# End of a mixed attention and expert kernel rearranged: stores ahead of the last heads, last sums inverted turned, last projection in parts, 71 expert tiles

## What is computed

```python
xn = layernorm(x)
# attention: 16 heads of 8 channels, rotary positions, causal
q, k, v = xn @ Wq.T, xn @ Wk.T, xn @ Wv.T
scores = q @ k.T / sqrt(8)                 # per head, upper triangle masked
att = softmax(scores) @ v
out_a = att @ Wo.T
# experts: 8, each row goes to its best two
probs = softmax(xn @ router_w.T);  top_w, top_idx = top_k(probs, 2)
top_w = top_w / (sum(top_w) + 1e-9)
h = relu(xn @ w1[e].T + b1[e]);  y = h @ w2[e].T + b2[e]
out_f = sum over the two of y * top_w
result = x + out_a + out_f
```

## Time and profile before

| | |
|---|---|
| median of 3 runs | 703.01 us (701.86 to 705.95) |
| the profiled execution | 699.11 us |
| its span, first to last instruction | 697.3 us |
| mean granted TensorE clock in it | 0.988 |
| busy: PE, PE weight loads, DVE, ACT, POOL | 93%, 54%, 80%, 66%, 37% |
| DMA | 69.34 MB, 99 GB/s over the span |

### The profile page before, as it was taken

The page is one execution under the profiler, slowest core; times in us unless marked ns, Lnnn a source line. Parts: engine busy times, 40 slices in busy tenths (PEclk is TensorE's granted clock), DMA queues, the critical chain, the costliest instruction groups (busy, mean ns, idle before and its releaser), DMA issues.

```text
span 697.3 us, 18181 instructions
## 1 busy us (share of the span) xinstructions
PE 651.8 (93%) x5925; PEld 376.8 (54%) x5925; DVE 554.9 (80%) x1306; ACT 463.3 (66%) x994; POOL 257.3 (37%) x308
## 2 busy tenths in 40 slices
PE   8699979999999999999999999999999998998995
PEld 3455534443443443447999999964344344343543
DVE  6956789999999798796666666679989988999424
ACT  3364207777778778777666666657777776777571
POOL 2556502217556556541000000024544544545350
PEclk9979999999999999999999999999999999999999
DMA  9499973146476355142322222271633626136034
GB/s 243 122 214 218 218 202 46 34 73 121 105 132 123 80 118 97 49 92 71 94 69 68 68 68 70 68 145 38 94 57 57 90 45 80 28 86 162 18 93 120
DMA packets 63660, 69.34 MB, mean 99 GB/s; under 512 B 8974, under 2 KB 51470, under 8 KB 63530
## 3 DMA queue, kind: packets, MB, share of 16 engines
q1 hardware_dynamic: 59464, 60.06, 39.5%
q0 software_dynamic: 4096, 8.40, 5.0%
q10 hardware_dynamic: 34, 0.02, 0.0%
HBM read 41.11 MB, written 26.67 MB: 97 GB/s over the span
## 4 chain that ended last, share of the span: by engine, by line
PE 34%; DVE 14%; issue 3%; DMA 3%; SPq 1%; ACT 0%; POOL 0%; DVEq 0%; POOLq 0%; ACTq 0%
PE bank L1441 9%; PE bank L1459 9%; DVE mx L922 9%; PE bank L1390 5%; PE bank L1355 4%; DVE q_high L914 3%; PE bank L1317 2%; DMA k_high<-slots_out_d,slot 1%; PE bank L1450 1%; PE bank L1485 1%; PE bank L1500 1%; DVE xn_all L1049 1%; DMA early<-heads_d 1%; DMA tiles_s<-heads_d 1%; PE bank L1325 1%
## 5 line engine op out<-in xcount | busy, mean ns | idle before, releaser
L794 ACT ACTIVATE probs<-bank 128x512 f32<-128x512 f32 (+2 forms) x640 | 319.3, 554 | 128.2 <-PE bank L1355 120.5
L922 DVE TENSOR_REDUCE mx<-bank 128x2 f32<-128x1024 f32 (+2 forms) x200 | 216.3, 1127 | 20.2 <-PE bank L1325 15.6
L689 POOL TENSOR_SCALAR_AFFINE_SELECT probs<-probs 128x512 f32<-128x512 f32 x128 | 83.6, 654 | 295.9 <-ACT probs L794 294.5
L1390 PE MATMUL bank<-probs,vst 128*32 128x256 f32 (+3 forms) x2432 | 187.0, 380 | 4.0 <-issue 2.9
L1355 PE MATMUL bank<-stack 64*128 64x512 f32 (+3 forms) x768 | 160.4, 417 | 1.3 <-ACT probs L794 0.7
L1317 PE MATMUL bank<-stack 64*128 64x512 f32 (+3 forms) x768 | 140.1, 382 | 16.2 <-DVE mx L922 9.3
L914 DVE CUSTOM_DVE_ANT_0 q_high<-bank,later_s 128x384 bf16<-128x384 f32 (+1 forms) x240 | 136.3, 618 | 17.7 <-PE bank L1317 15.9
L1355 PEld LDWEIGHTS bank<-stack 64*128 64x128 f32 x768 | 74.8, 185 | 110.6 <-ACT probs L794 90.7
L1317 PEld LDWEIGHTS bank<-stack 64*128 64x128 f32 x768 | 71.6, 185 | 59.0 <-DVE mx L922 32.6
L1390 PEld LDWEIGHTS bank<-probs,vst 128*32 128x32 f32 x2432 | 48.5, 108 | 78.0 <-issue 54.6
L672 POOL DMA_INDIRECT k_high<-slots_out_d,slot x64 | 61.3, 958 | 59.4 <-ACT probs L794 54.3
(11 more groups left out here) (138 smaller groups left out, 466.3 us busy)
## 6 DMA issues: line engine op xcount, KB each, us to landing
stack<-parts_d SPq DMA_DIRECT2D x96, 128.0 KB
slots_in_d<-const_s SPq DMA_DIRECT2D x4, 1152.0 KB, 10.6
tiles_s<-slots_in_d SPq DMA_DIRECT2D x72, 64.0 KB, 1.8
slots_out_d<-k_high SPq DMA_DIRECT2D x72, 64.0 KB, 1.6
early<-in_w_experts SPq DMA_DIRECT2D x8, 514.0 KB
stack<-parts_d SPq DMA_DIRECT2D x64, 64.0 KB
parts_d<-probs SPq DMA_DIRECT2D x8, 512.0 KB, 6.2
heads_d<-xnT SPq DMA_DIRECT2D x124, 18.0 KB
```

The source lines that it names most:

```text
L689: pool.affine_select(out=t, in_=t, compare_op=ALU.is_ge, fill=0.0, base=0, pattern=[[0, HG], [1, P]], channel_multiplier=-1).then_inc(s["d ...
L794: nc.scalar.activation(to, src, ACT.Exp, scale=SCALE).then_inc(s["probs_made"], 1)
L922: v.tensor_reduce(to, src.rearrange("p g (a k) -> p g a k", k=w), AX_X, ALU.max, negate=True).then_inc(s["scores_read"], 1)
L1390: last = mm(pv[32 * h:32 * h + 32, begin:end], vst[r % 2][:, kb, h, :], probs[n % 3][:, h, begin:end], start=first_of(n) and begin == 0, s ...
```

## The change

1. `TILES` is 71 instead of 72. With 8192 slots and 8 experts no more than 71 tiles can be in use. The loop over tiles makes 15 rounds of four instead of 16, and seven tiles are written out after it instead of four. The slots that are cleared, the counts that POOL waits for and the two late loads of `acc` (`ACC_AT`) follow.
2. SP issues the stores of sequences 0 and 1 before it stores the first half of unit 15, and it loads the last sequence's heads before it waits for the inverted sums.
3. The last sums are turned first: four matmuls with the 128x128 blocks of `oraw[1]` as weights and four columns give 128x16 in PSUM; DVE inverts 128x16, copies it out to 128x512 in two halves (each value 32 times), PE turns it back with the identity, and DVE multiplies from PSUM in two halves.
4. The last sequence's projection is in three parts of 4, 2 and 2 blocks of rows (`ENDS`), each in a bank of its own, with its own addition and its own store.
5. Their bias rows are issued inside unit 15, behind steps 6, 8 and 9 (`BIASED`), instead of at the end.

```diff
-TILES = SLOTS // P + E
+TILES = SLOTS // P + E - 1
...
-    with eng.Fori(1, TILES // 4 - 1) as i:
+    whole = (TILES - 4) // 4
+    with eng.Fori(1, whole) as i:
         for r in range(4):
             tile(i * 4 + r, r)
-    for r in range(4):
-        tile(TILES - 4 + r, r)
+    for j in range(4 * whole, TILES):
+        tile(j, j % 4)
...
+        ENDS = [(0, CK), (CK, CK + CK // 2), (CK + CK // 2, T)]
+
+        BIASED = {(LAST + 3, 6): 0, (LAST + 3, 8): 1, (LAST + 3, 9): 2}
...
-        ACC_AT = [0, 3, TILES - 4, TILES - 2]
+        ACC_AT = [0, 3, TILES - 3, TILES - 2]
...
+        def last_of_all(i):
+
+            use = place_in_order["project", B - 1, 0]
+            first, end = ENDS[i]
+            col = i % 2 * HALF
+            return ms[(use + i // 2) % 2][:, col:col + (end - first) * C]
...
+                if isinstance(u, int) and u == LAST + 3:
+                    for b in range(B - 2):
+                        store_out(b)
                 store_heads(u, 0)
...
                 if isinstance(u, int) and u == LAST + 3:
-                    for b in range(B - 2):
-                        store_out(b)
                     load_last_sums()
+                    load_last_heads()
                     spread_last()
                     store_out(B - 2)
...
-            dve.wait_ge(s["sums_spread"], 1)
-            v.reciprocal(over_last, st[0]).then_inc(s["over_made"], 1)
+            dve.wait_ge(s["sums_turned"], 1)
+            v.reciprocal(over_turned, st[0][:, 0:CK * HG]).then_inc(s["over_made"], 1)
             dve.wait_ge(s["over_made"], 1)
-            v.tensor_tensor(heads_last, oraw[1], over_last, ALU.mult).then_inc(s["att_ready"], 1)
-            for c in range(2):
-                dve.wait_ge(s["proj_made"], B + c)
+            for i in range(2):
+                some = slice(i * CK * HG // 2, (i + 1) * CK * HG // 2)
+                v.tensor_copy(over_wide[:, i * HALF // 2:(i + 1) * HALF // 2].rearrange("p (a r) -> p a r", r=32),
+                              over_turned[:, some].unsqueeze(2).broadcast_to([P, CK * HG // 2, 32])
+                              ).then_inc(s["turned_made"], 1)
+            for i in range(2):
+                dve.wait_ge(s["sums_spread"], i + 1)
+                cols = slice(i * HALF // 2, (i + 1) * HALF // 2)
+                v.tensor_tensor(heads_last[:, cols], oraw[1][:, cols], st[1 + i][:, 0:HALF // 2], ALU.mult
+                                ).then_inc(s["att_ready"], 1)
+            for i, (first, end) in enumerate(ENDS):
+                dve.wait_ge(s["proj_made"], B + i)
...
+            def bias_last(i):
+
+                use = place_in_order["project", B - 1, 0]
+                first, end = ENDS[i]
+                pe.wait_ge(s["scores_read"], use if i == 2 else use - 1)
+                pe.wait_ge(s["b2_loaded"], 16 * (NT // 2))
+                bt = (B - 1) % 2 * T
+                mm(last_of_all(i), gT[:, (B - 1) // 2, :],
+                   b2_blk[:, bt + first:bt + end, :].rearrange("p t c -> p (t c)"), start=True, stop=False)
...
-            mm(st[0], sum_rows, oraw[1], start=True, stop=True).then_inc(s["sums_spread"], 1)
...
+            pick_sums = sum_rows.rearrange("p (h r) -> p h r", h=HG)[:, :, 0]
+            for t in range(CK):
+                last = mm(st[0][:, t * HG:(t + 1) * HG], oraw[1][:, t * P:(t + 1) * P], pick_sums,
+                          start=True, stop=True)
+            last.then_inc(s["sums_turned"], 1)
+            for t in range(CK):
+                pe.wait_ge(s["turned_made"], 1 + t // 2)
+                last = mm(st[1 + t // 2][:, t % 2 * P:(t % 2 + 1) * P], over_wide[:, t * P:(t + 1) * P], ident,
+                          start=True, stop=True)
+                if t % 2:
+                    last.then_inc(s["sums_spread"], 1)
+            for i, n in ((0, H), (1, H - HG), (2, H - HG)):
+                pe.wait_ge(s["att_ready"], B + min(i, 1))
...
+            for i in (1, 2):
+                pe.wait_ge(s["att_ready"], B + 1 + i)
...
```

More of the change, by code:

```diff
@@ L412, in zero_slots @@
             def zero_slots(i):
-                tiles = slice(i * TILES // 4, (i + 1) * TILES // 4)
+                first, end = i * TILES // 4, (i + 1) * TILES // 4
+                tiles = slice(first, end)
                 sp.dma_start(slots_in_d.rearrange("(j p) c -> p j c", p=P)[:, tiles, :],
-                             zeros.unsqueeze(1).broadcast_to([P, TILES // 4, C])).then_inc(s["slots_zeroed"], 16)
+                             zeros.unsqueeze(1).broadcast_to([P, end - first, C])).then_inc(s["slots_zeroed"], 16)
             def load_stacks(u, r):
@@ L534, in spread_last, with load_last_heads, store_last @@
                         [n, DH, HALF])).then_inc(last_loaded[c], 16)
+            def load_last_heads():
+                for c, u in ((0, UNITS), (1, UNITS - 1)):
+                    n, cols = (u - LAST) * HG, slice(c * HALF, (c + 1) * HALF)
                     sp.dma_start(heads_s[B - 1][0:n * DH, cols], heads_d[LAST:u, :, 0:DH, cols].rearrange(
                         "g h d s -> (g h) d s")).then_inc(last_loaded[c], 16)
-            def store_last(c):
-                sp.wait_ge(s["scores_read"], place_in_order["project", B - 1, 0] + 1 + c)
+            def store_last(i):
+                first, end = ENDS[i]
+                sp.wait_ge(s["scores_read"], place_in_order["project", B - 1, 0] + 1 + i)
                 sp.wait_ge(s["combined"], 2 * NT)
-                t0 = (B - 1) * T + c * CK
-                sp.dma_start(out[t0 * P:(t0 + CK) * P, :].rearrange("(t p) c -> p t c", p=P),
-                             acc[:, t0:t0 + CK, :]).then_inc(s["out_stored"], 16)
+                t0 = (B - 1) * T + first
+                sp.dma_start(out[t0 * P:(t0 + end - first) * P, :].rearrange("(t p) c -> p t c", p=P),
+                             acc[:, t0:t0 + end - first, :]).then_inc(s["out_stored"], 16)
             def store_out(b):
@@ L598, in _ @@
             all_units(sp, unit, experts)
-            for c in range(2):
-                store_last(c)
-            sp.wait_ge(s["out_stored"], 16 * (B + 1))
+            for i in range(len(ENDS)):
+                store_last(i)
+            sp.wait_ge(s["out_stored"], 16 * (B - 1 + len(ENDS)))
         @block.gpsimd
@@ L1423, in unit @@
                         project(PROJECTS[u, j])
+                    if isinstance(u, int) and (u, j) in BIASED:
+                        bias_last(BIASED[u, j])
             LOADS = 2 * 6
@@ L1536, in _ @@
             pe.wait_ge(s["probs_made"], banks_before(UNITS, 0))
-            mm(st[0], sum_rows, oraw[1], start=True, stop=True).then_inc(s["sums_spread"], 1)
-            use = place_in_order["project", B - 1, 0]
-            at = ms[use % 2]
-            pe.wait_ge(s["scores_read"], use - 1)
-            for c, n in ((0, H), (1, H - HG)):
-                pe.wait_ge(s["att_ready"], B + c)
-                ps = at[:, c * HALF:(c + 1) * HALF]
-                bias_rows(ps, B - 1, c)
-                for t in range(CK):
-                    col = (c * CK + t) * P
-                    last = mm(ps[:, t * C:(t + 1) * C], heads_s[B - 1][0:n * DH, col:col + P],
-                              w_proj[0:n * DH, 5, :], start=False, stop=c == 0 and t == CK - 1)
-                if c == 0:
-                    last.then_inc(s["proj_made"], 1)
@@ L1552, in _ @@
-            pe.wait_ge(s["att_ready"], B + 2)
-            for t in range(CK):
-                last = mm(ps[:, t * C:(t + 1) * C], heads_last[:, t * P:(t + 1) * P], w_proj[:, 6, :],
-                          start=False, stop=t == CK - 1)
-            last.then_inc(s["proj_made"], 1)
+            pick_sums = sum_rows.rearrange("p (h r) -> p h r", h=HG)[:, :, 0]
+            for t in range(CK):
+                last = mm(st[0][:, t * HG:(t + 1) * HG], oraw[1][:, t * P:(t + 1) * P], pick_sums,
+                          start=True, stop=True)
@@ new lines, in _ @@
+            last.then_inc(s["sums_turned"], 1)
[7 more added lines that the diff above has]
+                pe.wait_ge(s["att_ready"], B + min(i, 1))
+                first, end = ENDS[i]
+                for t in range(first, end):
+                    to = last_of_all(i)[:, (t - first) * C:(t - first + 1) * C]
+                    last = mm(to, heads_s[B - 1][0:n * DH, t * P:(t + 1) * P], w_proj[0:n * DH, 5, :],
+                              start=False, stop=i == 0 and t == end - 1)
+                if i == 0:
+                    last.then_inc(s["proj_made"], 1)
@@ L1559 @@
+            for i in (1, 2):
+                pe.wait_ge(s["att_ready"], B + 1 + i)
+                first, end = ENDS[i]
+                for t in range(first, end):
+                    to = last_of_all(i)[:, (t - first) * C:(t - first + 1) * C]
+                    last = mm(to, heads_last[:, (t - CK) * P:(t - CK + 1) * P], w_proj[:, 6, :],
+                              start=False, stop=t == end - 1)
+                last.then_inc(s["proj_made"], 1)
```

14 lines of the change are left out of this document (6 added, 8 removed).

## The result

The changed kernel takes 699.21 us in the median of 15 runs (695.29 to 702.32), the kernel before 701.84 us over 15 runs (698.74 to 706.72; the three shown above are among them). The ratio on record, which is not the quotient of these two medians, is 0.9946 with a 95% interval of 0.9921 to 0.9970: 3.8 us faster (2.1 to 5.5), against 4.5 predicted. The medians alone differ by 2.6 us. The profiled execution took 697.34 us.

The account below looks back on a forecast made before the run. PE was taken to bound the expert phase, and a string of small transfers, with attention close beside it, the tail. From the 703.0 us median, −2.0 for the tile and −2.5 at the end gave 698.5 us; range 696.6 to 701.6.

Parts of the forecast that it names:

- the first case: Attention leads the transfers in the tail, as summed: 3.4 to 5.6 us faster, 697.4 to 699.6 us; chance 0.60.
- The tile: Expert phase, bound by PE: one loop round of four tiles becomes three written-out tiles, −2.01 us.
- The moved stores: SP's queue: outputs issued some 10 us earlier, so the sums' load lands in 2.17 instead of 3.67 us, −1.5.
- The other heads ready: Tail's transfer path: with heads loaded early, the other heads' second multiplication ends at 685.3 instead of 688.78 us.
- The bias rows: Unit 15: bias matmuls ahead of scores delay ACT by 1.1 us, bounds 0.3 and 1.7; the third costs nothing.
- The projection row: Profile evidence for the bias price: a projection's two halves take PE 3.5 us, and ACT then idled 4.11 us.
- From the second copy to the end: Last heads copied out at 686.3, then turning, small inversion, products, projection and last store; end at 694.7 or 694.8 us.
- The sum of the tail: Span ends at 694.7 or 694.8 instead of 697.3 us: −2.5 us for all tail edits together.
- The clock rival: PE's clock falls in the tail before the projection: +2.7 us, so −1.8 in all and 701.2 us; chance 0.20.
- Transfers leading: Tail's transfers stay last, other heads ready at about 688.7: −3.2 us in all, 699.8 us; chance 0.10.
- stores not hidden: Moved output stores hold up unit 15's gathers or code loads; ACT loses 3.0 us, 701.5 us; chance 0.06.
- the slower case: PE's clock falls before the last products, doubling the tail's matmuls: +5.9, so +1.4 and 704.4 us; chance 0.04.

Follow-up runs that it names:

- experiment 5: Changed kernel with SP's old order: outputs stored behind the last heads' stores, heads loaded beside the spread sums; 702.84 us in a single run.
- experiment 1: Kernel before with 71 tiles and nothing else of the change; 0.9955 of the kernel before.
- experiment 12: Kernel before with 71 tiles and SP's two queue moves, nothing else; 0.9915 of the kernel before, median 696.52 us.
- experiment 6: Rearranged kernel: changed kernel, small bias rows behind steps 9 and 10, large one and four other-heads matmuls in PE's tail pauses; 0.9906 of the kernel before.
- experiment 7: Changed kernel with eight filler matmuls among unit 0's first scores and PE's wait for the counts moved ahead of them; 0.9947 of the kernel before.
- experiment 11: Changed kernel again, unaltered; 0.9945 of the kernel before, median 698.55 us.
- experiment 2: Kernel before with SP's two queue moves alone, outputs stored and heads loaded earlier; 0.9963 of the kernel before.
- experiment 4: Changed kernel with the sums spread to 128x512 by one matmul and inverted at that width; 0.9911 of the kernel before.
- experiment 3: Changed kernel with its three bias matmuls moved out of unit 15 into PE's tail pauses; 0.9875 of the kernel before, 4 runs.
- experiment 10: Changed kernel with the three bias matmuls in PE's tail pauses, a second time; 0.9893 of the kernel before, median 695.12 us.

## Why the prediction came out right, and where its account was off

699.21 us lies in the first case's own range, 697.4 to 699.6, and 0.7 us over the forecast of 698.5. (By its own bounds, 0.6 us more for the bias and 0.3 for the tail, that range ends at 699.4.) That the time came so close is in part luck. The forecast subtracted from 703.01, the median of three runs; over 15 runs the kernel before is at 701.84, from which the same 4.5 us give 697.3. A base 1.2 us too high hid part of what the change fell short of. By its steps:

- **The tile**: −2.01 predicted, −2.05 measured (140.23 to 138.18), and again in every profile with 71 tiles. Right.
- **The moved stores**: the sums' load lands in 2.6 us in the changed kernel (2.2 to 2.9 in the eleven profiles with the new order) instead of 3.67, taken as 2.17 and announced as 2.0 to 2.4. The cause is right, the size 0.4 us too large. The wait for the heads' landing took the stores' place, 1.1 us, as said. What I under-priced is the other side: with the old order the landing took 4.92 and 5.05 us in experiments 5 and 1.
- **The other heads ready**: 15.2 us after the first copy predicted (685.3 − 670.1), 15.8 measured, with a combination's wait for its gather in between; in experiment 12, without that wait, 15.2. Attention led as forecast, by 1.85 us.
- **The bias rows**: 1.1 us taken, bounds 0.3 and 1.7, 1.5 measured in the first profile and 1.4 to 1.9 over all six. The projection row was the right neighbour, but the matmuls took 1.06 and 0.63 us of the chain where I had counted 0.86 and 0.43. The third one, costed at nothing, stands in the chain and yet costs nothing that shows: ACT idles no longer before the second copy than it did (2.10 and 2.13). It takes up PE's wait for the last mask, and two of them there no longer fit (experiment 6).
- **From the second copy to the end**: 9.1 predicted, 9.0 measured, step by step within 0.3 us, except that DVE's two copies took 0.49 us where I had counted about 0.8.
- **The sum of the tail**: −2.5 predicted, −2.3 measured, the difference being the bias rows. In the profiles of experiments 7 and 11, with the long mask, it would be −1.9 to −2.0 at full clock.

What the prediction got wrong is the account of what brings the gain. It put the tail's gain on the whole change, and said only in passing that what PE now does in series gives most of it back. Experiments 2 and 12 show all of it, 27.2 to 24.9, with the old code behind the new queue. From the second copy to the end experiments 2 and 12 take 10.6 and 10.5 us, experiment 4 (parts and early bias rows, old inversion) 9.9, and the changed kernel 9.0. So parts and early bias rows together gain 0.6 and the short inversion 1.0, and the unit gives 1.5 or more of it back. The rows for this were at hand. With attention leading, the old code goes from its copy's end at 685.18 through the sums' matmul (about 1.0, the wait in the last row above), 3.28, 0.69, 1.17, 0.69 and 2.59 to 694.6, 24.5 us after its first copy at 670.1: as short as the forecast tail of 24.7, with none of the new code. I never made that sum.

The clock rival had a chance of 0.20, as an alternative. It is rather a share: it struck two of three profiles of this tail, for 1.6 us from the second copy on, less than the 2.7 priced, since in experiment 11 it began at 687.3 and was over at 690.7, within the projection. With 0.5 to 1 us of it in a typical run the measured 3.8 against the 4.3 of the stages would be accounted for; two of three profiles are too few to call this shown. The page TensorE: Matmul & The Clock Gate of the Trainium skill, Part 1, says that half rate is the default state and that activity releases it. Experiment 5 agrees, where PE did nothing for 3 us before the fall. Most others settle nothing: in experiment 11 PE was busy for 1.9 of the 3.3 us before it, ahead of the fall at 106.9 for 2.2 of 2.8, and at 46 us, which the prediction calls agreement, PE was busy with narrow matmuls without a pause from 43.7 on (rows 8 and 10). Transfers leading and stores not hidden did not occur, nor did the slower case.

## What to carry to other kernels

When several edits to a tail are made together, ask what the cheapest of them does alone: here two moves in the order of a DMA queue gave all of what the tail gained, a large store that nobody waits for issued before a chain of small transfers, and loads issued while that chain waits. Work put into an engine's pause costs little as far as the pause reaches (0.1 to 0.2 us for three bias matmuls in experiments 3 and 10); beyond that, or in front of what a busy engine needs (a bias matmul ahead of scores for ACT), it passes on almost in full: 1.5 us of the 1.7 that two of them take. And where one profile differs by 3 us in a stretch that no edit touches, look at the granted clock there, and compare by stage between marks instead of by span.

## What the runs showed of the hardware

The granted clock fell at different places in executions of the same code, and this moves the kernel by several microseconds. Before the experts, where in PE's work no experiment but 7 differs, the first expert matmul comes between 320.1 and 323.5 us over all profiles. The stretch from experts to first copy is 208.0 to 210.3 us in ten profiles, and 211.7, 211.8, 212.4 and 212.9 in experiments 2, 5, 6 and 1, each of which has a low stretch of 3.4 to 6.8 us near 590 or 635 us. What such a stretch costs depends on its place: 10.2 us of it at 107 us cost 3.7, while experiment 2, with one as long from 88.9 us on, has its first expert matmul at 320.1, the earliest of all. A window of one of these (the rearranged kernel's first profile):

```profile
590.00:592.00 2.00, 2.00 (x16) 0.50 0.06 16
```

Runs of the kernel before on one chip lie 6 to 11 us apart (11 to 25 runs), twelve runs of the changed kernel 4.4. Taking pauses away in the tail helped in the sessions here; fillers at 104 us did not, and what would steady the first 120 us was not found.
